# A decoder layer with steps moved from VectorE to GpSimd and PSUM, and the orders of all engines laid anew

## The reference, cut to what matters

```python
h = layer_norm(x, ln1_w, ln1_b);  hh = time_shift(h)
xk, xv, xr = (h * m + hh * (1 - m) for m in (att_tmk, att_tmv, att_tmr))
k, v, sr = xk @ Wk.T, xv @ Wv.T, sigmoid(xr @ Wr.T)
rwkv = sr * wkv(time_decay, time_first, k, v)     # a scan: y = (e1*aa + e2*v) / (e1*bb + e2)
x = x + rwkv @ Wo.T
h = layer_norm(x, ln2_w, ln2_b);  hh = time_shift(h)
kk = square(relu(xk @ Wkey.T));  kv = kk @ Wval.T
x = x + sigmoid(xr @ Wrec.T) * kv
# between the heads of a token, causal over heads: q = layernorm(x), k = v = ctx
scores = einsum('bsqd,bskd->bsqk', q, k) / 4;  out = einsum('bsqk,bskd->bsqd', softmax(scores), v)
# low rank: (gelu((x @ U1) @ V1 + b1) @ U2) @ V2 + b2
```

## Time and profile before

| what | value |
|---|---|
| runs | 1237.48, 1244.14, 1268.12 us |
| median | 1244.14 us |
| the profiled execution | 1249.77 us, its span 1247.8 us |
| TensorE clock granted, mean | 0.945 |
| DMA, share of 16 engines | 9.5% |

### The profile page before, as it was taken

One profiled execution on the slowest core, in us unless ns is written; L12 is line 12 of the kernel. 1 busy time (PEld: TensorE's weight loads), 2 busy tenths in 40 slices (PEclk: granted clock), 3 DMA queues, 4 the chain that ended last, 5 costly groups with the idle time before them and its releaser, 6 DMA issues.

```text
span 1247.8 us, 14567 instructions
## 1 busy us (share of the span) xinstructions
PE 1032.6 (83%) x3584; PEld 584.6 (47%) x3584; DVE 1111.0 (89%) x2172; ACT 935.8 (75%) x2005; POOL 867.1 (69%) x783
## 2 busy tenths in 40 slices
PE   2679598989898989989798989989698998869515
PEld 1336263636455463736355463736346363626202
DVE  3755999999999999999999999999999999988681
ACT  4877779698888889796788879697688979464413
POOL 0112968788795968687595968688496968777680
PEclk9789799999999999999899999999899999979657
DMA  5010101001010101010010102001010101010000
GB/s 186 17 51 18 34 1 34 18 18 51 17 51 18 51 17 50 0 48 20 17 50 18 51 0 68 0 18 50 17 50 17 34 1 51 1 34 18 1 17 17
DMA packets 38964, 38.39 MB, mean 31 GB/s; under 512 B 2932, under 2 KB 38648, under 8 KB 38904
## 3 DMA queue, kind: packets, MB, share of 16 engines
q1 hardware_dynamic: 38904, 37.77, 9.5%
HBM read 29.38 MB, written 8.39 MB: 30 GB/s over the span
## 4 chain that ended last, share of the span: by engine, by line
PE 44%; DVE 32%; ACT 11%; issue 7%; POOL 4%; SPq 1%; DMA 0%; DVEq 0%; ACTq 0%; POOLq 0%
PE bank L813 19%; PE bank L870 8%; DVE x L1364 6%; PE bank L901 5%; DVE stat L1154 4%; PE bank L820 4%; PE bank L894 3%; DVE aa L1265 3%; PE bank L913 2%; DVE pp L1222 2%; POOL prod L338 2%; PE bank L885 2%; POOL prod L350 2%; DVE x L1306 2%; ACT n L462 2%
## 5 line engine op out<-in xcount | busy, mean ns | idle before, releaser
L338 POOL TENSOR_TENSOR prod<-q,kv_ctx 128x256 f32<-128x256 f32 (+5 forms) x448 | 394.7, 920 | 221.1 <-ACT q L462 221.1
L350 POOL TENSOR_TENSOR prod<-prob,v_dh 128x256 f32<-128x256 f32 (+3 forms) x256 | 390.9, 1568 | 29.2 <-ACT prob L564 29.2
L813 PE MATMUL bank<-xk,w_key 128*128 128x512 f32 x512 | 241.8, 612 | 17.6 <-DVE xk L1196 17.6
L870 PE MATMUL bank<-w_val,hidden 128*128 128x256 f32 x1024 | 225.9, 379 | 0.0
L870 PEld LDWEIGHTS bank<-w_val,hidden 128*128 128x128 f32 x1024 | 193.6, 190 | 32.4 <-issue 7.7
L1364 DVE TENSOR_REDUCE x<-prod 128x64 f32<-128x256 f32 (+3 forms) x256 | 189.9, 808 | 5.5 <-POOL prod L350 5.5
L1326 DVE TENSOR_REDUCE score<-prod 128x16 f32<-128x256 f32 (+5 forms) x448 | 175.5, 463 | 10.0 <-POOL prod L338 10.0
L813 PEld LDWEIGHTS bank<-xk,w_key 128*128 128x128 f32 x512 | 94.5, 194 | 141.8 <-issue 127.4
L548 ACT ACTIVATE hidden<-bank 128x512 f32<-128x512 f32 x128 | 74.9, 585 | 66.8 <-PE bank L813 66.7
L827 PE MATMUL bank<-ident,n 128*128 128x128 f32 x384 | 61.7, 297 | 75.5 <-ACT n L462 75.5
L422 ACT ACTIVATE lnv<-mv,eps_col 128x4 f32<-128x4 f32 x64 | 18.4, 287 | 127.2 <-DVE mv L1161 127.2
(11 more groups left out here) (96 smaller groups left out, 1946.4 us busy)
## 6 DMA issues: line engine op xcount, KB each, us to landing
x_in<-in_x SPq DMA_DIRECT2D x16, 512.0 KB, 3.6
kv_ctx<-in_ctx SPq DMA_DIRECT2D x16, 512.0 KB, 3.7
n<-in_x SPq DMA_DIRECT2D x16, 512.0 KB, 3.5
out<-y_out SPq DMA_DIRECT2D x16, 512.0 KB, 4.5
w_key<-in_wkey SPq DMA_DIRECT2D x1, 1024.0 KB
w_val<-in_wval SPq DMA_DIRECT2D x1, 1024.0 KB
w_k<-in_wk SPq DMA_DIRECT2D x1, 256.0 KB, 3.8
w_v<-in_wv SPq DMA_DIRECT2D x1, 256.0 KB, 4.2
```

Of the source, the lines that this page charges most:

```text
L338: ins = pool.tensor_tensor(o, a, b, ALU.mult)
L350: ins = pool.tensor_tensor(o, ph[:, HB * n:HB * n + HB, 0:keys].unsqueeze(2).to_broadcast(shape), vh[:, :, 0:keys].unsqueeze(1).to_broadca ...
L813: mm = pe.matmul(to[:, :], w[:, fi, P * f:P * f + P], src[:, fi, :], start=(fi == 0), stop=(fi == CH - 1))
L870: mm = pe.matmul(bank[6 + t // 2][:, C * (t % 2):C * (t % 2) + C], hidden[:, j, P * t:P * t + P], w_val[:, j, :], start=(j == 0), stop=(j ...
```

## The change

- The product of the gated numerator with the inverse denominator (`divide_num`) and the shift of the scores by their maximum (`shift_scores`) are GpSimd's instead of VectorE's.
- The factor e1 of the scans has no SBUF tile any more: `split_rise` and `exp_e1` write it into k's bank (0 and 1), and the scans read it there. `project_r`, which overwrites that bank, waits for `bb_done`.
- The value sums and their division by the mass are made in PSUM bank 5 (two token tiles at a time) and reach x3 in `third_residual` alone. For this `project_rec` and `transpose_4` use bank 4 for both halves.
- x isn't loaded again and added by VectorE: GpSimd issues one DMA with an adding write from the input tensor into x1 (`add_x`), after `normalise_2` and `stats_2` have read x1. `load_x_again` and `add_x_again` are gone, and `second_residual` waits for the DMA.
- ln 2 is taken into the logarithm (scale 2.0) instead of a bias of the exponential.
- `vec` is loaded ahead of the first x; `load_ctx` of a group is issued two steps later and waits for the value products of the group before the last.
- All orders are laid anew. VectorE's step begins with `sum_values(1)`, `over_mass` and `sum_values(2)` of group i-4, then `att_before_k` (both halves) and `att_before_v` of group i-1, `gate_values(0)` of group i-3, `scan_pp(0)`, `sum_values(3)`, `rise(0)`, `over_mass(1)`, `gate_values(1)`, `scan_pp(1)`, `first_residual(0)` of group i-2, `rise(1)`, `third_residual`, `stats_4`, `att_before_r(1)`, `mean_4`, `stats_2`, `weigh_token(0)`, a scan pair of aa, `first_residual(1)`, a scan pair of bb, `stats_2`, `weigh_token(1)`, `mean_2`, the other two scan pairs, `weigh_bonus` twice, `sum_scores(0)` of group i-3, `gate_num` twice, the rest of the score sums with `ffn_before_k/r` and `last_residual` among them, and `sum_values(0)`, `stats_1` and `sum_mass`. TensorE begins with `project_key` 2 to 7 of group i-3; one half of `project_k` now stands between `project_val` 1 and 2. ScalarE keeps the order of `normalise_2`, both `gate_of_r`, `copy_pT`, `ffn_now(0)`, four `gelu` and `ffn_now(1)`; one `copy_n4T` now stands within it.

The diff, cut to its core:

```diff
+            def add_x(g, par):
+
+                pool.wait_ge(n2_done, upto(g, 1))
+                pool.wait_ge(stats_read[2], upto(g, 2))
+                if some(g):
+                    pool.wait_ge(x_added, 16 * g)
+                pool.dma_start(x1[par][:, :, :], x_g[g], accum_op=ALU.add).then_inc(x_added, 16)
+
+            def shift_scores(g, s):
+                rows = slice(2 * NH * s, 2 * NH * s + 2 * NH)
+                pool.wait_ge(top_done, upto(g, 2, s + 1))
+                if some(g):
+                    pool.wait_ge(v_prod, upto(g - 1, 4, 2 * s + 2))
+                pool.tensor_tensor(prob[:, rows, :], score[:, rows, :],
+                                   top[:, rows].unsqueeze(2).to_broadcast([P, 2 * NH, NH]), ALU.subtract)\
+                    .then_inc(shift_done, 1)
...
+            def divide_num(g, f):
+                pool.wait_ge(gnum_done, upto(g, 2, f + 1))
+                pool.wait_ge(den_inv, upto(g, 2, f + 1))
+                pool.tensor_tensor(num[:, f, :], num[:, f, :], rr[:, f, :], ALU.mult).then_inc(rwkv_done, 1)
...
             def step(i, p, on):
...
+                if on(4):
+                    if on(5):
+                        pool.wait_ge(v_sum, upto(i - 5, 4))
+                    score_products(i - 4, p, 1, 1)
+                if on(2):
+                    add_aa(i - 2, 0)
+                    add_bb(i - 2, 0)
+                    add_aa(i - 2, 1)
...
+                    score_products(i - 4, p, 2, 2)
+                    shift_scores(i - 4, 0)
...
+                    score_products(i - 4, p, 3, 0)
...
+                    value_products(i - 4, 0, 1)
+                    shift_scores(i - 4, 1)
...
+                    value_products(i - 4, 1, 2)
...
+                    value_products(i - 4, 2, 0)
+                if on(3):
+                    add_x(i - 3, 1 - p)
...
+                    value_products(i - 4, 3, 1)
+                if on(2):
+                    add_bb(i - 2, 1)
+                    divide_num(i - 2, 0)
+                    divide_num(i - 2, 1)
...
+                    score_products(i - 3, 1 - p, 0, 0)
...
-                act.activation(e1[:, f, :], e1[:, f, :], ACT.Exp, scale=-1.0).then_inc(e1_exp, 1)
+                act.activation(bank[f][:, :], bank[f][:, :], ACT.Exp, scale=-1.0).then_inc(e1_exp, 1)
...
+                if on(1):
+                    pe.wait_ge(bb_done, upto(i - 1, 2, 1))
+                    project_r(i - 1, 0)
...
-                    ins = dve.tensor_tensor_scan(bb[:, SEQ * f + s, 1:T + 1], e1[:, f, cols],
+                    ins = dve.tensor_tensor_scan(bb[:, SEQ * f + s, 1:T + 1], bank[f][:, cols],
...
-                dve.wait_ge(res_done, upto(g, 1))
+                dve.wait_ge(x_added, 16 * (g + 1))
                 dve.scalar_tensor_tensor(out=pair(x2[par], s), in0=bank[6 + s][:, :], scalar=0.5,
                                          in1=pair(x1[par], s), op0=ALU.mult, op1=ALU.add).then_inc(x2_done, 1)
...
+                if t == 0 and some(g):
+                    dve.wait_ge(x3_done, upto(g - 1, 2))
+                if t == 2:
+                    dve.wait_ge(x3_done, upto(g, 2, 1))
...
+                    row = C * (t % 2) + HB * HD * n
+                    ins = dve.tensor_reduce(bank[5][:, row:row + HB * HD], src, AX.X, ALU.add)
...
+                dve.tensor_tensor(pair(x3[par], s), bank[5][:, :], pair(x2[par], s), ALU.add).then_inc(x3_done, 1)
```

More of the change, by code:

```diff
@@ L879, in transpose_4 @@
                 pe.wait_ge(n4_done, upto(g, 1))
-                transposes(bank[4 + f], f, n4, tr4_mm)
+                transposes(bank[4], f, n4, tr4_mm)
             def project_u1(g):
@@ new lines, in step @@
+                if on(1):
+                    if on(3):
+                        pe.wait_ge(relu_done, upto(i - 3, 8, 7))
+                    elif on(5):
+                        pe.wait_ge(y_done, upto(i - 5, 2, 1))
+                    elif on(2):
+                        pe.wait_ge(gnum_done, upto(i - 2, 2, 1))
+                    project_k(i - 1, 0)
+                if on(3):
+                    pe.wait_ge(xr2_done, upto(i - 3, 2))
+                    project_val(i - 3, 2)
+                    project_val(i - 3, 3)
@@ L1332, in top_scores @@
                 dve.tensor_reduce(top[:, rows], score[:, rows, :], AX.X, ALU.max).then_inc(top_done, 1)
-            def shift_scores(g, s):
-                rows = slice(2 * NH * s, 2 * NH * s + 2 * NH)
-                dve.wait_ge(top_done, upto(g, 2, s + 1))
-                if some(g):
-                    dve.wait_ge(v_prod, upto(g - 1, 4, 2 * s + 2))
-                dve.tensor_tensor(prob[:, rows, :], score[:, rows, :],
-                                  top[:, rows].unsqueeze(2).to_broadcast([P, 2 * NH, NH]), ALU.subtract)\
-                    .then_inc(shift_done, 1)
             def sum_mass(g, s):
@@ L1385, in step @@
             def step(i, p, on):
+                if on(4):
+                    sum_values(i - 4, 1, 2)
+                    inverse_mass(i - 4, 0)
+                    over_mass(i - 4, 0)
+                    inverse_mass(i - 4, 1)
+                if on(0):
+                    mean_1(i)
+                if on(4):
+                    third_residual(i - 4, p, 0)
+                    stats_4(i - 4, p, 0)
+                    sum_values(i - 4, 2, 0)
+                if on(1):
+                    att_before_k(i - 1, 0)
+                    att_before_k(i - 1, 1)
+                    att_before_v(i - 1, 0)
@@ new lines, in step @@
+                if on(3):
+                    gate_values(i - 3, 0)
+                if on(1):
+                    att_before_v(i - 1, 1)
+                    att_before_r(i - 1, 0)
+                if on(3):
+                    second_residual(i - 3, 1 - p, 0)
+                if on(1):
+                    scan_pp(i - 1, 0)
+                if on(4):
+                    sum_values(i - 4, 3, 1)
+                if on(1):
+                    rise(i - 1, 0)
+                if on(3):
+                    stats_3(i - 3, 1 - p, 0)
@@ new lines, in step @@
+                if on(4):
+                    over_mass(i - 4, 1)
+                if on(3):
+                    gate_values(i - 3, 1)
+                    second_residual(i - 3, 1 - p, 1)
+                    stats_3(i - 3, 1 - p, 1)
+                    mean_3(i - 3)
+                if on(1):
+                    scan_pp(i - 1, 1)
+                if on(2):
+                    first_residual(i - 2, p, 0)
+                if on(1):
+                    rise(i - 1, 1)
+                if on(4):
+                    third_residual(i - 4, p, 1)
+                    stats_4(i - 4, p, 1)
@@ L1386, in step @@
+                if on(1):
+                    att_before_r(i - 1, 1)
+                if on(4):
+                    mean_4(i - 4)
+                if on(2):
+                    stats_2(i - 2, p, 0)
+                if on(1):
+                    weigh_token(i - 1, 0)
+                    scan_aa(i - 1, 0)
+                if on(2):
+                    first_residual(i - 2, p, 1)
+                if on(1):
+                    scan_bb(i - 1, 0)
                 if on(2):
                     stats_2(i - 2, p, 1)
+                if on(1):
+                    weigh_token(i - 1, 1)
@@ L1456, in step @@
-                if on(1):
-                    divide_num(i - 1, 0)
-                if on(2):
-                    gate_values(i - 2, 1)
-                    second_residual(i - 2, p, 1)
-                    stats_3(i - 2, p, 1)
-                    mean_3(i - 2)
-                if on(1):
-                    divide_num(i - 1, 1)
-                if on(0):
-                    scan_pp(i, 0)
-                if on(3):
-                    over_mass(i - 3, 1 - p, 1)
-                if on(0):
-                    rise(i, 0)
```

588 lines of the change are left out of this document (234 added, 354 removed).

## The result

The changed kernel took 1201.19 us in the median (1200.23 to 1201.72, 4 runs), the kernel before 1246.16 on the same chip. The ratio is 0.966, its 95% interval 0.961 to 0.971: 3.4% faster. It is taken against the three faster of before's four runs (1237.5 to 1248.2; the fourth took 1268.1). The profiled execution has a span of 1199.4 us, 48.4 less than before.

A forecast was written before the change was run, and what follows sets the result against it. VectorE was taken as full before, a loop through TensorE as next: 68.0 us a step against 69.6 saves 23, with the drain 30, so span 1218; execution 1220, less the profiled run's 5.6 excess, gives 1214 us, range 1185 to 1255.

The forecast's parts named there:

- the drain: After mean_2 of group 15: 9.3 us less without the long stalls, of which GpSimd's shifts take back 2.5.
- the loop through TensorE: Path from mean_2 through TensorE back to mean_2, expected to set the step after the change: 68.0 us against 69.6.
- (1): Loop part from the end of mean_2 to the end of ffn_before_k(1): 14.9 us, not expected to shorten.
- (2): Loop part from there to the last project_val, TensorE nearly never idle: 37.4 us before, 39.3 forecast.
- (3): Loop part from gate_values(1) to the end of mean_2: 14.95 us before, 13.6 forecast.
- Fourteen equal steps: Steps from group 1 to group 15, each 1.6 us shorter: 23 us saved.
- VectorE's work: Sum of VectorE's edits over 16 groups: 168.5 us less, so 942.5 left, 58.9 a group.
- loop of "66 to 67": Loop through GpSimd's additions, scores, shifts and values and back through VectorE: 65.6 us, 66 to 67 with hand-overs.
- Rival A: The adding DMA's sum reaches second_residual late, deciding from a landing of 8 us; 1242 at 10, 1270 at 12; chance 0.14.
- Rival B: GpSimd becomes the bound through dearer shifts, DMA issue and waits: its loop grows to 69.5 us, time 1235; chance 0.21.
- Rival D: PSUM input leaves scans at 1.2 us and stalls on GpSimd remain: time 1235 us; chance 0.08.
- Rival C: Orders overlap better, ScalarE reaching ffn_now(1) earlier: 65 us a step, time 1172; chance 0.14.

The follow-up runs named there:

- rec_half: The changed kernel with the first half of project_rec working on half its input channels only (part of the computation left out): 1191.3 us.
- val_short: The changed kernel with GpSimd leaving out the last and largest of four value product instructions of token tile 2 in each group: 1199.1 us.
- scan_sbuf: The changed kernel with the scan factor e1 back in SBUF instead of PSUM: 1258.5 us.

## Why the prediction was right, and where its sizes were off

The span was forecast at 1218 and came out 18.6 shorter. The time was forecast at 1214 against 1201.2, and that this is nearer is luck: the 5.6 taken off for the profiled execution is scatter of the kernel before, and the changed kernel's profiled execution lies 0.1 from its median. Of the 25 us by which the steps were mis-sized, a longer fill and a smaller saving in the drain hide another 6.5. The mechanism held, the sizes less so.

- *What bounds before, and what is late next.* Right. The two steps of the kernel before that took 75.4 and 75.7 have one `over_mass` of 8.6 us each. (One of the three that it gives for one kind, the 12.78, is the addition of 128x1024, whose median is 1.46, and not of the form with 0.68.) VectorE is no longer full, and the loop through TensorE sets the step, shown by `rec_half`. The corners of the loop gave its three parts: (1) 14.9 forecast, 14.0 measured (396.04 to 410.03); (2) 39.3, measured 38.9 to 39.6; (3) 13.6, measured 13.6. Sum 68.0 against 66.8, with no hand-overs to add.
- *The term of the loop that was mis-sized most* is "so this part doesn't shorten" in (1). On ScalarE both `copy_n4T` stood in this stretch before (1.08 us in one row) and `copy_pT` waited 0.53 for TensorE; the new order has one copy there (0.59) and no wait. That is 1.0 by these rows, about the 0.9 that the part lost. I had read in the diff that one `copy_n4T` stays and priced it at nothing.
- *Fourteen equal steps.* The last step was counted as a regular one: it saves 6.1, and the 13 others save 3.24 each rather than 1.6. Of the 1.6 between these, 1.2 is the loop's size and 0.4 the kernel before: its 13 regular steps take 70.0 (group 14 ends at 1033.73), and 69.6 was a mean with the short last one. Together these are 25 us more than forecast. The prediction's 69.6 hid that the kernel before loses 13 us of its 13 regular steps in two of them. The fill gave 5.4 of them back (within the 5 that I had allowed, nearly), and the drain gave 5.7 where I had 6.8.
- *VectorE's work.* 942.5 forecast, 952.5 measured. The rows came at their prices: scans 80.2 for 84.4, `over_mass` 22.1 for 21.8, and the value sums in bank 5 take 2.9 more in all, within the 0.1 each that was allowed. Summed over its groups VectorE's time fell by some 167 us. The busy time fell less, since an instruction's row overlaps the next by some 0.08 us (442.22 to 442.90, the next at 442.82), and 80 of them are gone: 6 us that the sum should have had in it.
- *GpSimd.* Right in the sum: shift 1.07 for 1.25 and issue 1.14 for 1 to 2, but products 1.41 for 1.16, all in the mean; 56.3 us busy a group for 56.4 and the issue. The loop of "66 to 67" is 66.05 or less.
- *Rival A* is refuted by the 5.7 us to the landing; its mechanism is real, as the DMA one place later showed: 3.8 us of wait in a step, 63.5 us in all. The forecast put the limit at a landing of 8 us; `second_residual` starts 7.7 us after the issue (442.22 and 434.52), 2 us behind the landing. The Trainium skill's formula ("DMA: Bandwidth & Descriptors", Anatomy of one DMA) makes an estimated 3.2 of a plain load from GpSimd. The adding DMA measured here landed after 5.7, so the formula isn't to be used for an adding one.
- *Rival B* (GpSimd bound): refuted by `val_short`, though the sign that the prediction named for it came: VectorE waits 25.4 us in all for GpSimd before `sum_values`, 1.6 a step. Such a wait shows that the two paths meet there, and not which of them sets the step. *Rival D* (the PSUM input does nothing): refuted by `scan_sbuf` and by the over_mass rows in four kernels. *Rival C* (65 a step): its reason, ScalarE reaching `ffn_now(1)` sooner, is true for 0.9 us and no more.

What the prediction did not see is how much each move is needed. I priced them by VectorE's busy time, some 22 to 48 us each, and undoing one in the new orders costs more, except for the product: 57, 100, 112, 18.5 and 176 us, the clock's share included. The smaller edits of the change (ln 2, the place of the loads) were undone in no kernel of its own. The medians by orders and moves:

| | before's orders | new orders |
|---|---|---|
| no move | 1246.2 | 1352.3 |
| shift, product, adding DMA | 1399.5 | not run |
| these and the value sums | 1305.4 | 1258.5 |
| all five | not tried | 1201.2 |

The new orders lose without the moves, and before's orders lose with three or four of them. VectorE's two-SBUF-input steps are surely cheap only where they meet a gap in GpSimd's work; before's orders have such gaps for most of them, the new ones for fewer, and new work on GpSimd closes them in before's orders too. That all five moves in before's orders would lose as well is not shown: the factor in k's bank needs `scan_bb(1)` ahead of `project_r`, so another order of VectorE, and this was not tried.

## What to carry to other kernels

Price a VectorE step with two SBUF inputs by the run of GpSimd instructions that it may meet and by who waits behind it, not by its own busy time; with one input in PSUM such a step kept to its 0.67 to 0.69 us here, whatever GpSimd did. When work is moved onto an engine, look at what its gaps were letting through: an untouched instruction elsewhere may be the one that pays. And the clock granted to TensorE should be read beside every price of a wait. A sum over a loop should be made for both halves of an unrolled body, and the last step apart, and whether two paths tie is settled by shortening each, not by reading one step.

## What the runs showed of the hardware

- A VectorE instruction with two SBUF inputs can stand through a whole run of GpSimd instructions without a gap and end behind it: 8.84 us beside six instructions of three lines, 11.95 beside the rest of eight products and two additions, 6.00 to the last of fourteen. In the traces of the kernel before and of five experiments (the addition, the shift, the value sums, the new orders without moves, before's orders with three) 87 VectorE instructions took over 3 us. Of these, 81 ended 0.55 to 0.56 us (128x512) or 1.08 to 1.09 us (128x1024) after the first gap of GpSimd began; the other 6 ended inside a run.
- The short stalls are of another kind. Of the scans, `over_mass`, shifts and `third_residual` with two SBUF inputs, 270 took 1 to 3 us (the same traces and the one with the scan factor in SBUF), and 237 of them ended inside a run of GpSimd. So such a step often waits for little more than one GpSimd instruction (the longest takes 2.8 us), and sometimes for the whole run. What decides between the two is left open; in one kernel the same `over_mass` took 0.67 to 12.4 us.
- The Trainium skill ("SBUF — State Buffer", Who interferes with whom) says that such an instruction contends with GpSimd's reads, that the one to start first has the ports for the whole instruction, and that with at most one SBUF input (outside the two-port modes) there is no contention. The trace agrees on the last point (scans at 0.650 to 0.694 in the changed kernel, beside any work of GpSimd), and the short stalls fit a lock per instruction; the long ones are more than that.
- The clock granted to TensorE was lower in the kernels in which TensorE waits longer: 0.98 in the mean over thirteen steps of the changed kernel and 0.94 with the addition on VectorE. A 128x512 matmul of `project_key` has a median of 592 ns, and 1192 is the longest, at the lower of the two levels (1.2 instead of 2.4 GHz).
- An adding DMA of 512 KB issued by GpSimd held it for 0.99 to 1.42 us (median 1.14) and landed after 5.7, a plain one from SyncE after 3.5. In the kernels with this DMA GpSimd's next addition and first product were slower: 1.54 and 1.63 us in the changed kernel, with four value products between the issue and them, against 1.21 and 1.31 with the addition on VectorE. The product after a pause took 1.27 in both. What makes them slower is open.
